# Attention: key and query parts moved from the projection's tile to the score tiles within SBUF

## The reference

```python
x = x + xattn(layernorm(x), ctx, ctx, mask, wq, bq, wk, bk, wv, bv, wo, bo)
x = x + soft_moe(layernorm(x), ...)

def xattn(query, key, value, mask, ...):
    q = query @ wq + bq;  k = key @ wk + bk;  v = value @ wv + bv     # split into 16 heads
    score = einsum('bhqd,bhkd->bhqk', q, k) / sqrt(16) + (1 - mask) * -1e9
    alpha = softmax(score, axis=-1)
    return einsum('bhqk,bhkd->bhqd', alpha, v) @ wo + bo
```

## Time and profile before

| | us |
|---|---|
| median of 3 runs | 1098.72 (1097.23 to 1099.61) |
| profiled execution | 1100.38 |
| its span, first to last instruction | 1098.6 |

### The profile page before, as it was taken

How to read it: one execution, slowest core, us unless ns; L and a number is a source line. 1 busy time by engine, 2 the same in 40 slices (tenths; PEclk the granted TensorE clock), 3 DMA queues, 4 the chain that set the end, 5 groups by cost and what they waited for, 6 DMA issues and landing times.

```text
span 1098.6 us, 22347 instructions
## 1 busy us (share of the span) xinstructions
PE 1008.0 (92%) x7440; PEld 673.5 (61%) x7440; DVE 790.1 (72%) x1379; ACT 591.1 (54%) x1052; POOL 423.1 (39%) x477
## 2 busy tenths in 40 slices
PE   4778999999987798988999999999999999999996
PEld 3566677777764455545666666656666666666664
DVE  4647777777767677766878787787777787877754
ACT  1457687878763777864443444443534435444421
POOL 5248776767674433338323042032141230420000
PEclk8879999999997999999999999999999999999999
DMA  7957777878651544454335144252442352442122
GB/s 206 177 117 147 151 168 157 162 158 156 141 132 54 173 104 110 128 137 144 88 83 161 39 106 143 44 160 74 107 136 60 82 161 39 112 137 46 28 69 80
DMA packets 122162, 128.38 MB, mean 117 GB/s; under 512 B 49556, under 2 KB 110472, under 8 KB 122072
## 3 DMA queue, kind: packets, MB, share of 16 engines
q1 hardware_dynamic: 108016, 85.51, 35.1%
q0 software_dynamic: 10896, 40.61, 12.4%
q10 hardware_dynamic: 3160, 1.11, 0.6%
HBM read 80.22 MB, written 29.96 MB: 100 GB/s over the span
## 4 chain that ended last, share of the span: by engine, by line
PE 53%; DVE 1%; issue 1%; ACT 1%; DVEq 0%; ACTq 0%
PE down L1869 15%; PE second L1292 15%; PE up L1292 7%; PE gate L1292 7%; PE mix L1815 5%; PE mix L1808 3%; PE mix L1805 0%; DVE hid_l L1704 0%; DVE x L1675 0%; ACT hid_h L1786 0%; DVE gate_sb L1692 0%; ACT wgu_h L1368 0%; DVE wd_l L1712 0%; ACT gate_sb L1769 0%; ACT slot_h L1755 0%
## 5 line engine op out<-in xcount | busy, mean ns | idle before, releaser
L421 POOL TENSOR_TENSOR p_l<-p_f,p_h 121x800 f16<-121x800 f32 (+1 forms) x96 | 163.6, 1720 | 77.0 <-ACT p_h L695 76.2
L527 DVE TENSOR_REDUCE head_max<-at_rows 100x2 f32<-100x722 f32 x124 | 112.9, 911 | 70.5 <-PE at_rows L773 68.9
L1786 ACT ACTIVATE hid_h<-gate_sb,hid_scale 128x512 f16<-128x512 f32 x128 | 91.9, 718 | 100.7 <-DVE gate_sb L1692 100.5
L1869 PE MATMUL down<-wd_h,hid_h 128*128 128x256 f16 x512 | 139.4, 272 | 4.7 <-DVE hid_l L1704 4.4
L1869 PE MATMUL down<-wd_h,hid_l 128*128 128x256 f16 x512 | 139.5, 272 | 0.0
L1869 PE MATMUL down<-wd_l,hid_h 128*128 128x256 f16 x512 | 139.5, 272 | 0.0
L1769 ACT ACTIVATE gate_sb<-gate,bgu,un_gate 128x512 f32<-128x512 f32 x63 | 48.8, 775 | 148.2 <-PE gate L1292 148.2
L1704 DVE SCALAR_TENSOR_TENSOR hid_l<-gate_sb,hid_scale,hid_h 128x512 f16<-128x512 f32 x128 | 99.6, 778 | 20.9 <-ACT hid_h L1786 17.2
L690 ACT ACTIVATE p_f<-at_cols 121x800 f32<-121x800 f32 (+1 forms) x96 | 79.6, 829 | 25.6 <-PE at_cols L795 24.6
L1356 POOL DMA_DIRECT2D bd<-in_bd x16 | 9.0, 560 | 209.3 <-DVE eo L1726 209.3
L695 ACT ACTIVATE p_h<-p_f 121x800 f16<-121x800 f32 (+1 forms) x96 | 83.6, 871 | 3.0
(11 more groups left out here) (203 smaller groups left out, 2492.5 us busy)
## 6 DMA issues: line engine op xcount, KB each, us to landing
eo_pair<-eo SPq DMA_DIRECT2D x128, 128.0 KB, 2.7
k_parts<-kq_n SPq DMA_DIRECT2D x16, 724.0 KB, 3.7
kt<-k_parts SPq DMA_DIRECT2D x32, 362.0 KB
wgu<-in_Wg POOLq DMA_DIRECT2D x16, 512.0 KB, 5.5
wgu<-in_Wu POOLq DMA_DIRECT2D x16, 512.0 KB, 7.3
wd<-in_Wd POOLq DMA_DIRECT2D x16, 512.0 KB, 6.8
combine<-combT SPq DMA_DIRECT2D x16, 400.0 KB, 3.6
dispatch<-dispT SPq DMA_DIRECT2D x16, 400.0 KB
```

What stands on the lines that cost most here:

```text
L421: nc.gpsimd.tensor_tensor(p_l[i][0:kn, :, 0:N], p_f[i][0:kn], p_h[i][0:kn, :, 0:N], ALU.subtract).then_inc(p_low, 1)
L527: nc.vector.tensor_reduce(head_max[:, :, r], bank[0:N, :, 0:S], AX.X, ALU.max).then_inc(max_ready, 1)
L1786: nc.scalar.activation(hid_h[:, c, :], gate[c % 2][:], ACT.Copy, scale=keep["hid_scale"][:, bass.ds(ex, 1)]).then_inc(hidh_ready, 1)
L1869: mm = nc.tensor.matmul(down_ps[t // 2][:, t % 2, :], ht[:, c, t * P:(t + 1) * P], wt[:, c, :], start=(c == 0 and k == 0), stop=(c == FC - ...
```

## The change

The stores of key and query parts to DRAM and the loads from there are gone. In their place SP moves each part of each half directly from `kq_n` into its 16 partitions of `kt` or `qt`: six DMAs for the keys, six for the queries, each from 128 partitions. They are issued at the end of the step in which the parts are made, after the row maxima and the context load, where the stores stood; in the fill step t = -1 the row maxima of element 0 now come ahead of element 2's moves, and the context of element 3 after them. The mask rows still come from DRAM, after the key moves. The writers of `kq_n` wait for the moves (`k_moved`, with the masks counted in, and `q_moved`), and so does the first score matmul.

```diff
-KQ_LOADS = 10
+K_MOVES, Q_MOVES = 8, 6
...
-    def load_queries(queue, b, t):
+    def move_queries(queue, b, t):
...
-        if 0 <= t < B:
-            queue.wait_ge(st_done, NHALF * (b + 1))
         if t < 0:
             queue.wait_ge(qt_set[i], 32)
-        queue.wait_ge(q_stored, 16 * p + 16)
+        else:
+            queue.wait_ge(st_done, NHALF * (b + 1))
+        queue.wait_ge(q_lo, 2 * p + 2)
         for c in range(2):
             cols = slice(N * c, N * c + N)
-            both = q_dram[i][c, :, :, 0:N].rearrange("r (d h) n -> (r d) h n", d=HD)
-            queue.dma_start(qt[i][HEAD_ROWS * c + HD:HEAD_ROWS * c + 3 * HD, :, cols].bitcast(F32), both).then_inc(kq_in[i], 16)
...
+            for slot_of, part in ((0, 0), (1, 0), (2, 1)):
+                row = HEAD_ROWS * c + HD * slot_of
+                queue.dma_start(qt[i][row:row + HD, :, cols].bitcast(F32), kq_n[:, c, part, SW:SW + N].bitcast(F32)).then_inc(q_moved, 16)
...
-        def store_keys(b, t):
-            sp.wait_ge(k_lo, 2 * b + 8)
-            sp.dma_start(k_dram[(t + 3) % NBUF][:, :, :, 0:SW].rearrange("c r p k -> p (c r) k"),
-                         kq_n[:, :, :, 0:SW].rearrange("p c r k -> p (c r) k").bitcast(F32)).then_inc(k_stored, 16)
...
-        def load_keys(b, t):
+        def move_keys(b, t):
...
+            sp.wait_ge(k_lo, 2 * p + 2)
+            for c in range(2):
+                for slot_of, part in ((0, 0), (1, 1), (2, 0)):
+                    row = HEAD_ROWS * c + HD * slot_of
+                    sp.dma_start(kt[i][row:row + HD, :, :].bitcast(F32), kq_n[:, c, part, 0:SW].bitcast(F32)).then_inc(k_moved, 16)
             for c in range(2):
                 rows = slice(HEAD_ROWS * c + ROW_MASK, HEAD_ROWS * c + HEAD_ROWS)
                 sp.dma_start(kt[i][rows, :, :].bitcast(F32), at(mask_dram, p).rearrange("r (o k) -> r o k", o=1).broadcast_to([2, NPAIR, SW])
-                             ).then_inc(kq_in[i], 16)
-            sp.wait_ge(k_stored, 16 * p + 16)
...
+                             ).then_inc(k_moved, 16)
...
         def fill_step(b, t):
-            if t >= -2:
-                load_keys(b - 1, t - 1)
...
             if t == -1:
-                load_queries(sp, b - 1, t - 1)
                 sp.dma_start(x_all[:, 4:B], x[4:B].rearrange("b n d -> n b d")).then_inc(x_in[1], 16)
-            store_keys(b, t)
-            store_queries(b, t)
+                max_rows(b, t)
+            move_keys(b, t)
+            if t >= -2:
+                move_queries(sp, b, t)
             if t == -1:
-                max_rows(b, t)
                 next_ctx(b, t)
...
         def step(b, t, trip):
...
-            if 0 <= t + 2 < B:
-                load_keys(b - 1, t - 1)
-            if 0 <= t + 2 < B:
-                load_queries(sp, b - 1, t - 1)
             if 0 <= t + 1 and t + 4 < B:
                 next_ctx(b, t)
             if 0 <= t + 1 < B:
                 max_rows(b, t)
             if 0 <= t + 3 < B:
-                store_keys(b, t)
-            if 0 <= t + 3 < B:
-                store_queries(b, t)
+                move_keys(b, t)
+                move_queries(sp, b, t)
...
                         if t >= -2:
-                            act.wait_ge(k_stored, 16 * p)
+                            act.wait_ge(k_moved, 16 * K_MOVES * p)
                         nc.scalar.activation(kq_n[:, c, 0, 0:S], k_ps[c], ACT.Identity, bias=bk[:, c:c + 1]).then_inc(k_hi, 1)
...
-                    pe.wait_ge(kq_in[(t + 1) % NBUF], 16 * KQ_LOADS * (turn + 1))
+                    pe.wait_ge(k_moved, 16 * K_MOVES * (m + 1))
+                    pe.wait_ge(q_moved, 16 * Q_MOVES * (m + 1))
```

More of the change, by code:

```diff
@@ L34 @@
 SW = S + 1
-K_ROW, Q_ROW = 368, 112
 KC, NKC = 121, 3
@@ L206, in attention_phase @@
     k_hi, k_lo, q_hi, q_lo = sem("k_hi"), sem("k_lo"), sem("q_hi"), sem("q_lo")
-    k_stored, q_stored, kq_in = sem("k_stored"), sem("q_stored"), [sem(f"kq_in{i}") for i in range(NBUF)]
+    k_moved, q_moved = sem("k_moved"), sem("q_moved")
     v_hi, v_res, v_mid, v_lo = sem("v_hi"), sem("v_res"), sem("v_mid"), sem("v_lo")
@@ L294, in next_ctx @@
             load_ctx(b + 4, (t + 4) % NBUF)
-        def store_keys(b, t):
-            sp.wait_ge(k_lo, 2 * b + 8)
-            sp.dma_start(k_dram[(t + 3) % NBUF][:, :, :, 0:SW].rearrange("c r p k -> p (c r) k"),
-                         kq_n[:, :, :, 0:SW].rearrange("p c r k -> p (c r) k").bitcast(F32)).then_inc(k_stored, 16)
[L301 to L304, removed]
-        def load_keys(b, t):
+        def move_keys(b, t):
             p, i = b + 3, (t + 3) % NBUF
-            if 0 <= t < B:
-                sp.wait_ge(st_done, NHALF * (b + 1))
             if t < 0:
                 sp.wait_ge(kt_set[i], 1)
+            else:
+                sp.wait_ge(st_done, NHALF * (b + 1))
+            sp.wait_ge(k_lo, 2 * p + 2)
[3 more added lines that the diff above has]
+                    sp.dma_start(kt[i][row:row + HD, :, :].bitcast(F32), kq_n[:, c, part, 0:SW].bitcast(F32)).then_inc(k_moved, 16)
             for c in range(2):
@@ L315, in load_keys @@
                 sp.dma_start(kt[i][rows, :, :].bitcast(F32), at(mask_dram, p).rearrange("r (o k) -> r o k", o=1).broadcast_to([2, NPAIR, SW])
-                             ).then_inc(kq_in[i], 16)
-            sp.wait_ge(k_stored, 16 * p + 16)
-            for c in range(2):
-                both = k_dram[i][c, :, :, 0:SW].rearrange("r (d h) k -> (r d) h k", d=HD)
-                sp.dma_start(kt[i][HEAD_ROWS * c:HEAD_ROWS * c + 2 * HD, :, :].bitcast(F32), both).then_inc(kq_in[i], 16)
-            for c in range(2):
-                high = k_dram[i][c, 0, :, 0:SW].rearrange("(d h) k -> d h k", d=HD)
-                sp.dma_start(kt[i][HEAD_ROWS * c + 2 * HD:HEAD_ROWS * c + 3 * HD, :, :].bitcast(F32), high).then_inc(kq_in[i], 16)
+                             ).then_inc(k_moved, 16)
         def fill_step(b, t):
-            if t >= -2:
-                load_keys(b - 1, t - 1)
             if t == -2:
@@ L578, in part @@
                 if t >= -2:
-                    dve.wait_ge(q_stored, 16 * p)
+                    dve.wait_ge(q_moved, 16 * Q_MOVES * p)
                 for c in range(2):
@@ L732, in step @@
             if t == -2:
-                load_queries(act, b - 1, t - 1)
+                move_queries(act, b - 1, t - 1)
             for s in range(SLOTS):
@@ L761, in scores @@
                 if r == 0:
-                    turn = trip + (t + 1) // NBUF
-                    pe.wait_ge(kq_in[(t + 1) % NBUF], 16 * KQ_LOADS * (turn + 1))
+                    pe.wait_ge(k_moved, 16 * K_MOVES * (m + 1))
+                    pe.wait_ge(q_moved, 16 * Q_MOVES * (m + 1))
                     if t >= 0:
```

10 lines of the change are left out of this document (2 added, 8 removed).

## The result

| | median us | ratio to before, 95% interval |
|---|---|---|
| before, beside it | 1098.89 (1094.69 to 1107.91, 20 runs) | |
| after | 1105.68 (1099.90 to 1114.07, 20 runs) | 1.0045 [1.0023, 1.0067] |
| after, timed again beside the experiments | 1106.28 (1101.39 to 1111.29, 12 runs) | 1.0056 [1.0027, 1.0085] |

By the ratios the change makes the kernel about 5 to 6 us slower. The forecast was 1098.0, 0.7 us faster, so about no change: the time lies in the range, but it moved the other way, to the side that had the chance of 0.26. The profiled execution took 1107.82 us (span 1105.9).

What follows compares the result with a forecast made beforehand. Steady attention was taken as bound by compute engines waiting for each other, not by DMAs. The terms -1.5 + 0.9 - 0.5 + 0.4 = -0.7 us, on the median 1098.72, gave 1098.0; range 1094 to 1108.

Steps and rivals of the forecast that it cites:

- the side that had the chance of 0.26: Whole kernel: the chance that the change makes it slower; faster had 0.30, same 0.44.
- The time of the moves: Moves into 16 partitions: 107 GB/s, 1.73 us each, 10.4 us for an element's keys, data 0.9 us after issue.
- The steady state: Steady attention, 17.86 us a step: no cost or gain; moves end 2 us before ACT wants kq_n.
- Element 0: Fill: keys and queries share the engines until 32.2, ACT's keys of element 1 wait to 32.0, chain 2.0 us late.
- The wait for the maxima: Fill: TensorE's 3.59 us idle for the maxima's DMA, after element 1's second score matmuls, was to go.
- The last element's wait for its queries: End of attention: the first scores' 0.47 us wait was to go, saving between 0 and 0.5; 0.5 taken.
- Element 1 "just covered": Fill: ACT's keys of element 2 wait to 46, but DVE took them only at 46.6, so no further delay.
- The gain of 1.5 us at the maxima: Fill: transposed scores start at 57.8 instead of 59.34, held by the second score matmuls; 1.5 us gained.
- The context, 0.9 us: Fill: element 3's context load, behind element 2's moves, lands at 70.7; its projection, due at 69.8, waits 0.9 us.
- the clock: Fill, TensorE idling longer around 30 us: a lower granted clock could cost 0.9 us or nothing; 0.4 taken.
- The rival with slower moves: Moves slower than the loads, kq_n late in every step: 1114 at 78 GB/s, about 1103 near the threshold; chance 0.22.

Runs made afterwards that it cites:

- own tile: Changed kernel with element 0's key and query parts in a tile of their own, so element 1's writers don't wait: 1100.98 us, ratio 1.0000.
- the four groups: The experiments were timed in four groups, the unedited kernel before beside each: medians 1101.12, 1100.21, 1102.83 and 1101.08 us.
- context first: Changed kernel with element 3's context load issued ahead of element 2's moves: 1100.53 us, ratio 0.9987; timed again 1100.60, ratio 0.9995.
- masks apart: Changed kernel with the two mask DMAs on semaphores of their own, for which only the scores wait: 1104.80 us, ratio 1.0028.
- the gap filled: Five spare matmuls in TensorE's gap before the router's last transposes: changed kernel 1105.29 us (ratio 1.0049), with context load ahead of moves 1100.55, kernel before 1101.56.
- the three edits together: Changed kernel with element 0's own tile, the context load ahead of the moves, and masks on their own semaphores: 1098.06 us, ratio 0.9986.
- context and masks: Changed kernel with the context load ahead of element 2's moves and the masks on semaphores of their own: 1099.32 us, ratio 0.9987.

## Why the prediction was wrong

Right were these steps. The time of the moves: six in 11.48 us against 11.3 (107 GB/s taken, 116 to 125 measured, with later first data and a later release that make up for it). The steady state: no gain and nearly no loss, although the 2 us to spare were in fact used up (ACT's keys came 13.34 us after the moves' issue, just when they became free). Element 0: ACT's keys of element 1 at 14.04 us after the first move by the forecast, 14.10 measured; DVE's at 14.5, measured 14.7. That one is luck too: the forecast ended this wait with keys and queries together, while with the masks apart the keys alone let ACT go after 12.0 us (30.70 - 18.72); the masks made up the rest. The wait for the maxima is gone in the first trace (0.88 us are left in the second).

The last element's wait for its queries is gone as well, but not the 0.5 us that the forecast took for it, since the same scores now wait about as long for DVE:

```profile
317.68 0.54 PE L748 MATMUL at_rows<-kt,qt 100*100 100x362 f32 x2 [0.42 <-DVE max_p L581]
```

Wrong were three terms, all in the fill.

1. *Element 1 "just covered".* The forecast ended ACT's wait with the last key move and let the masks "follow on two engines" at no cost, though the change counts them in `k_moved`, and it let data start 0.9 us after issue, where they took 1.4 (issue at 195.63 in the step above, first window with data at 197.0). It had DVE's low parts of element 2 at 28.6 us after the first key move; they came at 30.75. That is 13.37 us for a set that alone takes 11.5, and put the first mark at 36.0, not 33.5.

2. *The gain of 1.5 us at the maxima.* It was used up by the first: the second score matmuls come at 59.97 - 19.37 = 40.6 us, before at 36.9, and the transposed scores right behind them start 60.69 - 19.37 = 41.32 us after the first key move, before at 59.34 - 17.96 = 41.38. The gain was 0.

3. *The context, 0.9 us, and the clock.* This is the term that makes the sign. With element 2's moves issued 38.9 us after the first key move instead of 36.4, the context came behind them so late that the projection began at 54.55 instead of the 52.7 forecast. TensorE, at the upper level of its clock, stood ready at 50.55 instead of 51.8, so the wait was 4.0. The clock that fell behind it is priced in the forecast at 0.4, for the stretch around 30 us alone; in this execution it cost 1.4 on the second mark and 1.3 on the step after it, counted against the changed kernel's second trace. The 1.3 is not the wait's alone, as kernels without the wait had it too (last part).

In the terms of the forecast: the projection that needs the context was to stand 0.6 us earlier than before (-1.5 + 0.9) and stands 1.2 later (54.55 against 71.33 - 17.96 = 53.37); the clock 2.7 for 0.4; the rest of attention, from the third mark to the last, 0.5 for -0.5. In sum 4.4 for -0.7, and the last mark is 315.3 - 310.8 = 4.5 us late. The timed loss is 5 to 6.

So what failed is the forecast's account of the fill: it had element 1 just covered, a gain of 1.5 us at the maxima and 0.9 us for the context. Element 1 came 2.1 us late, the gain was 0, and the wait for the context was 4.0.

That the context's place costs the timed loss is shown by two pairs of kernels that differ in it alone and were timed side by side (5.7 and 4.7 us between the two orders, the context ahead level with before). Their marks differ by only 2.0 to 3.4 us, though, and the own tile was level with before with the context still behind. The granted clock of the runs goes along with most of the difference. Among the runs of the kernel before, and of the changed kernel, a mean clock lower by 0.001 goes with a time longer by 0.65 to 0.9 us, and the changed kernel's runs had the lower clock. The last column is an estimate: the time read at a clock of 0.977 off a straight line through each kernel's timed runs.

| kernel | median granted clock | median us | at 0.977 |
|---|---|---|---|
| before, in the four groups | 0.976 to 0.978 | 1100.21 to 1102.83 | 1100.7 to 1101.1 |
| after; again | 0.973; 0.9735 | 1105.68; 1106.28 | 1103.2; 1104.2 |
| context first; again | 0.9775; 0.976 | 1100.53; 1100.60 | 1100.2; 1100.7 |
| masks apart | 0.9735 | 1104.80 | 1101.5 |
| own tile for element 0 | 0.978 | 1100.98 | 1101.6 |

At an equal clock 2 to 3.5 us of the loss remain, about what the last marks show (1.8 and 4.5 us over before), and 2.5 to 4 us between the two orders. The rest of the 5 to 6 goes with the lower clock of the changed kernel's runs. With the gap filled its median clock was 0.977. Whether the change lowers the clock, and in which stretch of the runs that have no trace, stays open.

The rival with slower moves named the sign but not the cause: the moves were as fast as forecast. No rival had the context in it; the forecast itself had, at 0.9 us.

## What to carry to other kernels

When an edit reorders a queue, follow the one transfer that it puts last as closely as those it takes away: here 361 KB behind 1.4 MB cost more than anything that the change took away had saved, with the moves' time priced right. A semaphore is as late as the smallest and last thing counted in it, so count only what the waiter needs. And a wait that vanishes at one place may come back at the next, so follow the next transfer in the same queue to its reader before counting a gain.

## What the runs showed of the hardware

Moves within SBUF, from 128 partitions into 32, ran at 130 GB/s, hardly above the 119 into 16 (both after about a microsecond above 200), while loads from DRAM into 32 had 200. For the moves into 16 and 32 the next DMA was issued some 1.5 us after the last packets, for those into 128 some 0.3 us. And TensorE's clock has a say in each execution of the fill. From 72 to 84 us the granted clock was 1.00 in the profiled executions of before, after again, context first again and the three edits together, and there the step from the second mark to the third took 18.8 us; it fell to between 0.57 and 0.95 in windows of 4 us of that stretch in after, context first, masks apart, context and masks, and own tile, and the same step took 20.0 to 20.1, with a wait for the context ahead of it or without one.
